# First u product of batch 2 split inside the last expert unit, tile 10 reordered, and the start of a fused attention and mixture-of-experts kernel rearranged

## The chip, the cores and the metric

The kernel runs on one core of one Trainium2 chip. The metric is the device time of one execution in microseconds (us). Engines are named as the profile names them: PE is TensorE, ACT is ScalarE, DVE is VectorE, POOL is GpSimd, SP the engine that issues most DMAs.

## What is computed

```python
xn = layernorm(x)                                  # x: 4 batches x 1024 tokens x 256
q, k, v = xn @ Wq.T + bq, xn @ Wk.T + bk, xn @ Wv.T + bv
qk = q @ k.T                                       # per batch, unscaled
theta = 0.5 + 0.2 * sigmoid(qk) + 0.15 * tanh(qk) + 0.1 * relu(qk)
s = (softmax(theta) @ v) @ Wo.T + bo
e = argmax(xn @ Wr + br)                           # one of 8 experts
y = gelu(xn @ W1[e] + b1[e]) @ W2[e] + b2[e]       # 256 -> 1024 -> 256
out = x + s * silu(y)
```

## The kernel before

**Work.** A tile is 128 tokens: 32 tiles, 8 to a batch. Large products are made of rounded parts, high and low: three matmuls (lines 899, 900, 901, in `product`) stand for one. `M` (from Wq and Wk) turns xn into u, and scores are u times xn; `G` (from Wv and Wo) turns xn into v. Every result of PE lands in one of eight banks of PSUM. ACT copies it out as the high part (`high_u`, `high_v`), DVE subtracts that to get the low part (`low_u`, `low_v`); only then may PE use it, or overwrite the bank.

**Stages.** (1) The start: DVE takes row statistics (`row_statistics`, `variances`, `scales`), three engines normalize tiles, PE turns them (`turn_0`), `first_u` makes u of batch 0, and the router's logits of batch 0 come from `route_0`. (2) Attention of batch 0, while the other batches are normalized on POOL, turned (`turn`) and routed. (3) Experts: the tokens, sorted by expert, pass in units of 256 rows. A unit that is at most half full takes another path: `half_rows`, `half_turned` and `half_out` on PE, `gelus_half` on ACT, `parts_half` on DVE. (4) Attention of batches 1 to 3, tiles 8 to 31, which begins inside the last units of the experts. In this execution the last unit (338 to 348.5 us) is a half one, and so is the only unit of expert 6 (304.4 to 313.9 us).

**A tile n of stage 4.** PE: `scores(n + 1)`; a wait for the low parts of tile n - 1's transposed weights (`pT_ready`); `transposes(n)`; a job; `weighted(n - 1)`, the product with v. ACT: six activations of tile n + 1 (`acts`), the transposed copy of tile n (`transposed_high`), two exponentials of tile n + 1 (`exps`), then the job's high part. DVE: `thetas(n + 1)`, `transposed_parts(n)`, the job's low part, and `finish(n - 1)`, which divides and frees the bank of `values`.

**Jobs.** `next_job(n)` gives for tile n a piece of the next batch's u (four) or v (four). All jobs of batches 2 and 3 use bank 7, so each waits until the piece before has both parts (`u_ready`). The first, for tile 9, is not run by the loop on PE but in the last expert unit, ahead of `half_turned`. Its parts, though, are made by the loop's turn of tile 9, behind `exps(10)` on ACT and `transposed_parts(9)` on DVE. The next job, of tile 10, waits for them.

**Order.** Every engine's program is written out by hand and runs in order; semaphores hold an instruction until its inputs are there, and all that stands behind it on that engine waits too. In the experts' stage each engine branches on the number of units, which it reads at run time.

Of the kernel before, what the change touches and what calls it, by code (L numbers as in the profile page):

```python
# [17 lines left out]
def block_attention_moe(nc, x, Wq, bq, Wk, bk, Wv, bv, Wo, bo, Wr, br, W1, b1, W2, b2, out):  # L18
# [34 lines left out]
    with ExitStack() as ctx:  # L53
# [496 lines left out]
        def _(act):  # L550
# [111 lines left out]
            act.wait_ge(scales_ready, 1)  # L662
            normalize(range(2))
            for m in range(DC):
# [130 lines left out]
            def units_of(e, u0, full, u1):  # L795
# [4 lines left out]
                with act.If(u0 < full):  # L800
                    gelus(u0, par)
                    row_high(u0 + 1)
                    high_w1(w1_landed, other, raw[0], slice(0, 1))
                with act.If(full < u0 + 1):
                    gelus_half(u0, par, beside=lambda: high_w1(w1_landed, other, raw[0], slice(0, 1)))
                    row_high(u0 + 1)
# [58 lines left out]
            with act.If(last_u < u7 + 2):  # L865
                tile_8()
            nc.scalar.activation(warm[:, 3:4], zeros[:, 0:1], ACT.Gelu)
            with act.If(last_u < full_7):
                gelus(last_u, 1)
            with act.If(full_7 < last_u + 1):  # L870
                gelus_half(last_u, 1)

# [7 lines left out]
            for n in range(TPB + 1, NT):  # L880
                if n + 1 < NT:
                    acts(n + 1, 0)
                    acts(n + 1, 1, beside=(lambda: transposed_high_0(NT - 2)) if n == NT - 2 else None)
                    transposed_high(n)
                    exps(n + 1)
                    job = next_job(n)
                    if job:
                        (high_u if job[0] == "u" else high_v)(*job[1:])
                    if n in ROWS_AT:
                        high_xT(3, [ROWS_AT.index(n)])  # L890
                else:
                    transposed_high(n)

        @block.tensor
        def _(pe):
# [225 lines left out]
            for m in range(DC):  # L1121
                for ec in range(DC):
                    last = mm(ps[:, 7, m * D:(m + 1) * D], wv_raw[:, ec, m * P:(m + 1) * P], woT[:, ec, :],
                              start=ec == 0, stop=ec == DC - 1)
                    if m == DC - 1 and ec == DC - 1:
                        last.then_inc(G_done, 1)
                    route_0(4 + 2 * m + ec)
            for ec in range(DC):
# [207 lines left out]
            for n in range(TPB + 1, NT - 1):  # L1336
# [3 lines left out]
                if n == TPB + 1:  # L1340
                    wait_apart(pe, y_biased, end_of[E - 1])
                    weighted(n - 1)
                    transposes(n)
                else:
                    pe.wait_ge(pT_ready, n * 2)
# [13 lines left out]
        def _(dve):  # L1359
# [137 lines left out]
            dve.wait_ge(scales_ready, 1)  # L1497
            normalize(range(2, 3))
            dve.wait_ge(x0_in[1], 16)
            statistics = row_statistics(range(4, TPB))  # L1500
            dve.wait_ge(biasT_done, 1)
            v.tensor_copy(bias_cols[:, :], ps[:, 6, BIAS_COL:BIAS_COL + 3 * DC]).then_inc(bias_kept, 1)
            step(statistics)
            variances(4, TPB)
# [57 lines left out]
            def take_turned(i):  # L1562
# [6 lines left out]

            thetas(0, [0])  # L1570
            dve.wait_ge(x_in[2], 16)
            row_statistics(range(2 * TPB, 2 * TPB + 2))
            dve.wait_ge(G_high, 1)
            v.tensor_tensor(G_lo[:, :, :], pair_of(ps[:, 7, :]), G_hi[:, :, :].bitcast(F32), ALU.subtract
# [11 lines left out]
                                   ).then_inc(const_kept, 1)  # L1586
            row_statistics(range(2 * TPB + 2, 3 * TPB))
            dve.wait_ge(x_in[1], 16)
# [165 lines left out]
            def first_unit_of(u, full, e, par):  # L1754

                other = 1 - par
                with dve.If(u < full):
                    hidden_parts(u)
                    row_low(u + 1)
                    low_w1(e, other, 0)  # L1760
                with dve.If(full < u + 1):
                    parts_half(u, beside=lambda: low_w1(e, other, 0))
                    row_low(u + 1)
# [80 lines left out]
            def job(n):  # L1844

                if next_job(n):
                    kind, b, q = next_job(n)
                    (low_u if kind == "u" else low_v)(b, q)
                if n in ROWS_AT:
                    low_xT(3, [ROWS_AT.index(n)])  # L1850

            thetas(TPB + 1)
            biased(last_u, 1)
# [68 lines left out]
```

## Time and profile before

| | us |
|---|---|
| median of 3 runs | 527.67 |
| lowest and highest | 527.51, 527.84 |
| the profiled execution | 527.64 |
| its span, first to last instruction | 525.6 |

| engine | busy us | share of the span |
|---|---|---|
| PE, matmuls | 515.6 | 98% |
| PE, weight loads | 484.3 | 92% |
| DVE | 402.6 | 77% |
| ACT | 344.6 | 66% |
| POOL | 195.8 | 37% |

A busy share is an average over all stages. Matmuls overlap, so a row's length is not its cost: a 128x512 matmul is shown with 0.39 us, but the next one starts 0.23 us later. Costs on PE are taken from start to start. PE's granted clock is 1.00 of full speed in every stretch used here.

### The profile page before, as it was taken

The page shows a single profiled execution, that of the slowest core. Times are in us where ns is not written, and L with a number is a line of the kernel's source. Part 1 is how long each engine was busy: PE and PEld are TensorE (multiplying, and loading weights), DVE is VectorE, ACT ScalarE, POOL GpSimd, SP SyncE. Part 2 cuts the span into 40 slices and gives each one's busy share as a digit, 9 for nine tenths or more (in the row PEclk, how much of TensorE's full clock was granted, in tenths as well). Part 3 has the DMA queues.
Part 4 walks back from the last instruction along what each step waited for, and adds up shares of the span by engine and source line. Part 5 has one row for each costly group of instructions (what it writes and reads, how often), then busy time and mean ns, then how long its engine had stood idle before and what let it go on. Part 6 is the DMA issues. An engine that isn't in the chain of part 4 may idle for free.

```text
span 525.6 us, 10829 instructions
## 1 busy us (share of the span) xinstructions
PE 515.6 (98%) x3773; PEld 484.3 (92%) x3773; DVE 402.6 (77%) x811; ACT 344.6 (66%) x633; POOL 195.8 (37%) x227
## 2 busy tenths in 40 slices
PE   7999999999999999999999989999999999999997
PEld 6899998899989999899999979998999989999997
DVE  5898689946578855598555688768999998867887
ACT  4789778437356733466343575899787786777884
POOL 3218419913112222222112222005676785342441
PEclk9999999999999999999999999999999999999999
DMA  8964720031635711247311421005233232211221
GB/s 266 344 225 176 285 81 1 2 120 32 230 123 151 255 55 41 61 133 237 112 40 40 136 70 42 21 22 190 62 99 113 71 114 87 62 44 49 60 71 51
DMA packets 40754, 57.49 MB, mean 109 GB/s; under 512 B 3654, under 2 KB 35788, under 8 KB 40156
## 3 DMA queue, kind: packets, MB, share of 16 engines
q1 hardware_dynamic: 35452, 46.02, 26.5%
q0 software_dynamic: 3488, 9.47, 6.4%
q10 hardware_dynamic: 1760, 1.32, 0.8%
q8 instruction: 28, 0.46, 0.4%
q14 instruction: 26, 0.21, 0.1%
HBM read 41.07 MB, written 17.56 MB: 112 GB/s over the span
## 4 chain that ended last, share of the span: by engine, by line
PE 86%; ACT 6%; DVE 5%; issue 1%; POOL 1%; DMA 1%; ACTq 0%; DVEq 0%
PE ps L899 26%; PE ps L901 25%; PE ps L900 25%; PE ps L1014 5%; DVE stats L1375 2%; PE ps L1193 1%; PE ps L1080 1%; ACT hid L763 1%; POOL xn_all L464 1%; DMA xn_all<-in_L_attn_x_dram 1%; PE ps L1070 1%; ACT relu_s L628 1%; ACT tanh_s L625 1%; ACT theta L624 1%; PE ps L1045 1%
## 5 line engine op out<-in xcount | busy, mean ns | idle before, releaser
L899 PE MATMUL ps<-v_hi,pT_hi 128*128 128x258 f32 x256 | 74.9, 293 | 0.2
L747 ACT ACTIVATE hid<-ps,b_now 128x256 f32<-128x256 f32 x128 | 53.7, 472 | 29.7 <-PE ps L901 28.8
L900 PE MATMUL ps<-v_lo,pT_hi 128*128 128x258 f32 x256 | 72.5, 283 | 0.0
L901 PE MATMUL ps<-v_hi,pT_lo 128*128 128x258 f32 x256 | 72.3, 282 | 0.0
L1430 DVE SCALAR_TENSOR_TENSOR theta<-tanh_s,theta 128x512 f32<-128x512 f32 x64 | 47.3, 739 | 23.5 <-ACT tanh_s L625 22.9
L899 PE MATMUL ps<-w_hi_even,hidT_h 128*128 128x256 f32 x200 | 58.5, 293 | 1.6 <-DVE hidT_l L1727 1.1
L636 ACT ACTIVATE theta<-theta,neg_max 128x512 f32<-128x512 f32 x64 | 43.0, 720 | 24.9 <-DVE neg_max L1436 24.6
L519 POOL COPY unit_token<-sorted_token 128x2 int32 x19 | 4.5, 238 | 142.9 <-PE ps L1193 142.9
L901 PE MATMUL ps<-w_hi_even,hidT_l 128*128 128x256 f32 x200 | 56.6, 283 | 0.0
L900 PE MATMUL ps<-w_lo_even,hidT_h 128*128 128x256 f32 x200 | 56.6, 283 | 0.0
L778 ACT ACTIVATE g_sb<-y_sb 128x512 f32<-128x512 f32 x20 | 12.6, 631 | 65.8 <-DVE y_sb L1742 65.8
L624 ACT ACTIVATE theta<-ps,c_half 128x512 f32<-128x512 f32 x64 | 44.3, 692 | 17.4 <-PE ps L901 17.3
L510 POOL DMA_INDIRECT row<-xn_rows,unit_token x38 | 44.1, 1161 | 20.7 <-POOL unit_token L519 14.9
L899 PE MATMUL ps<-xnT_hi,u_hi 128*128 128x512 f32 x128 | 51.7, 404 | 0.0
L526 POOL DMA_INDIRECT g_tile<-sorted_g,slot_g x32 | 37.5, 1171 | 38.0 <-DMA sorted_g<-g_sb 32.7
L901 PE MATMUL ps<-xnT_hi,u_lo 128*128 128x512 f32 x128 | 50.4, 394 | 0.0
L900 PE MATMUL ps<-xnT_lo,u_hi 128*128 128x512 f32 x128 | 50.0, 391 | 0.0
L899 PEld LDWEIGHTS ps<-v_hi,pT_hi 128*128 128x128 f32 x256 | 48.4, 189 | 1.7 <-issue 1.2
L901 PE MATMUL ps<-rowT_h,w_lo_even 128*128 128x256 f32 x176 | 49.8, 283 | 0.0
L899 PE MATMUL ps<-rowT_h,w_hi_even 128*128 128x256 f32 x176 | 49.8, 283 | 0.0
L900 PE MATMUL ps<-rowT_l,w_hi_even 128*128 128x256 f32 x176 | 49.8, 283 | 0.0
L900 PEld LDWEIGHTS ps<-v_lo,pT_hi 128*128 128x128 f32 x256 | 48.6, 190 | 0.3
(258 smaller groups left out, 1641.5 us busy)
## 6 DMA issues: line engine op xcount, KB each, us to landing
w_raw_odd<-in_L_ffn_W_dram SPq DMA_DIRECT2D x10, 1024.0 KB
w_raw_even<-in_L_ffn_W_dram SPq DMA_DIRECT2D x6, 1024.0 KB
sorted_g<-g_sb SPq DMA_DIRECT2D x20, 256.0 KB, 2.2
xn_rows<-xn_all SPq DMA_DIRECT2D x4, 1024.0 KB, 6.2
x_tile<-in_L_attn_x_dram SPq DMA_DIRECT2D x32, 128.0 KB, 2.2
out_dram<-g_tile SPq DMA_DIRECT2D x32, 128.0 KB, 1.7
xn_all<-in_L_attn_x_dram SPq DMA_DIRECT2D x3, 1024.0 KB, 12.4
kept_xT<-passing_xT SPq DMA_DIRECT2D x2, 1024.0 KB, 4.0
```

Source lines behind the costliest of these rows:

```text
L510: pool.indirect_dma_start(row[:, a, :], None, xn_rows, bass.IndirectOffsetOnAxis(ap=tokens[:, a:a + 1], axis=0)).then_inc(row_in, 16)
L526: pool.indirect_dma_start(g_tile[:, p % RING, :], None, sorted_g, bass.IndirectOffsetOnAxis(ap=slot_g[:, n:n + 1], axis=0)).then_inc(g_in[ ...
L624: nc.scalar.activation(theta[:, j % 2, cols], bank, ACT.Tanh, bias=c_half[:, n:n + 1], scale=0.5)
L636: nc.scalar.activation(part, part, ACT.Exp, bias=neg_max[:, j % 2, 1:2], scale=-1.0, accum_out=exp_sums[:, h:h + 1] if n == NT - 1 else No ...
L747: last = nc.scalar.activation(hid[:, j % 2, c * UNIT:(c + 1) * UNIT], ps[:, HID_BANK + j, c * UNIT:(c + 1) * UNIT], ACT.Gelu, bias=b1_now[ ...
L778: nc.scalar.activation(g_sb[:, :, :], y_sb[:, :, :], ACT.Tanh, scale=0.5).then_inc(y_tanh, 1)
L899: mm(dst, a_hi, b_hi, start=first, stop=False)
L900: mm(dst, a_hi, b_lo, start=False, stop=False)
L901: return mm(dst, a_lo, b_hi, start=False, stop=last)
L1014: last = nc.tensor.transpose(pT_bank(n, h)[:, i * P:(i + 1) * P], theta[:, n % 2, h * HALF + i * P:h * HALF + (i + 1) * P], ident[:, :])
L1375: last = v.bn_stats(stats[:, i, :], xn_all[:, i, :])
L1430: v.scalar_tensor_tensor(part, tanh_s[:, cols], KT, part, ALU.mult, ALU.add).then_inc(mixed, 1)
```

## The change

Six edits, no arithmetic among them.

1. The parts of job 9 (u of batch 2, piece 0): ACT's `high_u` goes into the last unit, in a half one between the copy of `hid` and the GELUs; DVE's `low_u` goes behind the last unit's parts, ahead of `thetas(9)`.
2. PE at tile 10: the job now stands ahead of the wait and of the transposes.
3. ACT and DVE at each expert's first unit: the second `If` becomes an `Else`.
4. The first rows: ACT normalizes tile 0 alone, DVE tiles 1 and 2 (it was 0 and 1, and 2). DVE's statistics of tiles 4 to 7 come behind the copy of the bias columns.
5. PE: the logits of tiles 4 to 7 come in one group behind all four products of `G`, whose semaphore is raised at the end of these.
6. DVE: statistics of two tiles of batch 2 move ahead of `thetas(0, [0])`, so that two fewer remain for later.

```diff
@@ ACT
-            normalize(range(2))
+            normalize(range(1))
...
-                with act.If(full < u0 + 1):
+                with act.Else():
                     gelus_half(u0, par, beside=lambda: high_w1(w1_landed, other, raw[0], slice(0, 1)))
...
+            def first_job():
+                high_u(*next_job(TPB + 1)[1:])
             with act.If(last_u < full_7):
                 gelus(last_u, 1)
+                first_job()
             with act.If(full_7 < last_u + 1):
-                gelus_half(last_u, 1)
+                gelus_half(last_u, 1, beside=first_job)
...
-                    if job:
+                    if job and n > TPB + 1:
@@ PE
-                    if m == DC - 1 and ec == DC - 1:
-                        last.then_inc(G_done, 1)
-                    route_0(4 + 2 * m + ec)
+            last.then_inc(G_done, 1)
+            for t in range(4, TPB):
+                route_0(t)
...
+                elif n == TPB + 2:
+                    job(n)
+                    pe.wait_ge(pT_ready, n * 2)
+                    transposes(n)
+                    weighted(n - 1)
@@ DVE
-            normalize(range(2, 3))
-            dve.wait_ge(x0_in[1], 16)
-            statistics = row_statistics(range(4, TPB))
+            normalize(range(1, 3))
             dve.wait_ge(biasT_done, 1)
             v.tensor_copy(bias_cols[:, :], ps[:, 6, BIAS_COL:BIAS_COL + 3 * DC]).then_inc(bias_kept, 1)
-            step(statistics)
+            dve.wait_ge(x0_in[1], 16)
+            step(row_statistics(range(4, TPB)))
...
-            thetas(0, [0])
             dve.wait_ge(x_in[2], 16)
             row_statistics(range(2 * TPB, 2 * TPB + 2))
+            thetas(0, [0])
+            row_statistics(range(2 * TPB + 2, 2 * TPB + 4))
...
-                with dve.If(full < u + 1):
+                with dve.Else():
...
-                if next_job(n):
+                if next_job(n) and n > TPB + 1:
...
+            low_u(*next_job(TPB + 1)[1:])
             thetas(TPB + 1)
```

What this does to the engines' programs at three places:

PE at tile 10, before. The rows are the end of `scores(11)`, the transposes (`ident,theta`), the job (`M_hi`, `M_lo`) and the first of `weighted(9)`.

```order
L901 MATMUL ps<-xnT_hi,u_lo 128x512
L1014 MATMUL ps<-ident,theta 128x128 x8
L899 MATMUL ps<-xnT_hi,M_hi 128x512
L900 MATMUL ps<-xnT_lo,M_hi 128x512
L901 MATMUL ps<-xnT_hi,M_lo 128x512
...
L899 MATMUL ps<-v_hi,pT_hi 128x258
```

The same place after:

```order
L905 MATMUL ps<-xnT_hi,u_lo 128x512
L903 MATMUL ps<-xnT_hi,M_hi 128x512
L904 MATMUL ps<-xnT_lo,M_hi 128x512
L905 MATMUL ps<-xnT_hi,M_lo 128x512
...
L1014 MATMUL ps<-ident,theta 128x128 x8
L903 MATMUL ps<-v_hi,pT_hi 128x258
```

The job's six matmuls moved ahead of the eight transposes.

ACT in the last unit and at tile 10, before: the half unit's copy, GELUs and parts; left out are tile 9's and tile 10's activations; then the exponentials of tile 10 and the high part of u.

```order
L757 ACTIVATE hid<-ps 128x512
L761 REGISTER_ALU
L763 ACTIVATE hid<-ps,b_now 128x128 x4
...
L636 ACTIVATE theta<-theta,neg_max 128x512 x2
L585 ACTIVATE u_hi<-ps,r_col 128x512
L624 ACTIVATE theta<-ps,c_half 128x512
```

The same places after:

```order
L757 ACTIVATE hid<-ps 128x512
L585 ACTIVATE u_hi<-ps,r_col 128x512
L761 REGISTER_ALU
L763 ACTIVATE hid<-ps,b_now 128x128 x4
...
L636 ACTIVATE theta<-theta,neg_max 128x512 x2
L624 ACTIVATE theta<-ps,c_half 128x512
```

`u_hi` moved from behind tile 10's exponentials to behind the half unit's copy.

DVE at the start, before: normalizing the first rows, the statistics of tiles 4 to 7, the copy of the bias columns, the variances.

```order
L1390 SCALAR_TENSOR_TENSOR shift<-mean_var,rstd 128x4
L1484 TENSOR_SCALAR xn_all<-xn_all,rstd,shift 128x256
L1375 BN_STATS stats<-xn_all 128x6 x4
L1502 COPY bias_cols<-ps 128x6
L1382 BN_AGGR mean_var<-stats 128x2 x4
```

After:

```order
L1399 SCALAR_TENSOR_TENSOR shift<-mean_var,rstd 128x4
L1493 TENSOR_SCALAR xn_all<-xn_all,rstd,shift 128x256 x2
L1509 COPY bias_cols<-ps 128x6
L1384 BN_STATS stats<-xn_all 128x6 x4
L1391 BN_AGGR mean_var<-stats 128x2 x4
```

One more tile is normalized here, and the four statistics moved behind the copy, which waits for a transpose of PE.

## Rows read from the trace of the kernel before

**Rows 1.** The page, busy time: us, share of the span, instructions.

```profile
PE 515.6 (98%) x3773; PEld 484.3 (92%) x3773; DVE 402.6 (77%) x811; ACT 344.6 (66%) x633; POOL 195.8 (37%) x227
```

**Rows 2.** Timeline of PE at tile 10: start, us, engine, line, instruction, idle before.

```profile
358.43 0.39 PE L901 MATMUL ps<-xnT_hi,u_lo 128*128 128x512 f32 x1
359.11 1.09 PE L1014 MATMUL ps<-ident,theta 128*128 128x128 f32 x8 [0.29 <-DVE pT_lo L1451]
360.63 0.50 PE L899 MATMUL ps<-xnT_hi,M_hi 128*128 128x512 f32 x1 [0.43 <-DVE u_lo L1410]
...
362.13 0.28 PE L899 MATMUL ps<-v_hi,pT_hi 128*128 128x258 f32 x1
```

**Rows 3.** Timelines of PE, ACT and DVE in the last unit, ACT at tile 10.

```profile
341.71 0.39 PE L901 MATMUL ps<-xnT_hi,M_lo 128*128 128x512 f32 x1
...
341.32 0.58 ACT L757 ACTIVATE hid<-ps 128x512 f32<-128x512 f32 x1
342.65 0.63 ACT L763 ACTIVATE hid<-ps,b_now 128x128 f32<-128x128 f32 x2 [0.75 <-PE ps L1248]
...
359.13 0.67 ACT L585 ACTIVATE u_hi<-ps,r_col 128x512 fp32r<-128x512 f32 x1
...
346.86 0.69 DVE L1430 SCALAR_TENSOR_TENSOR theta<-tanh_s,theta 128x512 f32<-128x512 f32 x1 [0.70 <-ACT tanh_s L625]
```

**Rows 4.** Timelines of DVE, POOL and PE around tile 11.

```profile
362.80 0.85 DVE L1430 SCALAR_TENSOR_TENSOR theta<-tanh_s,theta 128x512 f32<-128x512 f32 x1 [0.29 <-ACT tanh_s L625]
363.68 1.12 DVE L1436 CUSTOM_DVE_ANT_0 theta<-theta,relu_s,neg_max 128x512 f32<-128x512 f32 x1
...
365.44 1.29 DVE L1451 TENSOR_TENSOR pT_lo<-ps,pT_hi 128x512 fp32r<-128x512 f32 x2
366.79 0.75 DVE L1410 SCALAR_TENSOR_TENSOR u_lo<-ps,r_col,u_hi 128x512 fp32r<-128x512 f32 x1
...
362.03 1.07 POOL L543 TENSOR_TENSOR g_tile<-half_s,g_tile 128x256 f32<-128x256 f32 x1 [0.85 <-DMA g_tile<-sorted_g,slot_g]
363.18 1.07 POOL L546 TENSOR_TENSOR g_tile<-g_tile,x_tile 128x256 f32<-128x256 f32 x1
...
367.76 1.03 PE L1014 MATMUL ps<-ident,theta 128*128 128x128 f32 x8
368.55 0.48 PE L899 MATMUL ps<-xnT_hi,M_hi 128*128 128x512 f32 x1
```

**Rows 5.** Chain of waits at expert 6's half unit, then PE's timeline there.

```profile
306.93 0.04 ACTq L804
...
306.99 0.04 ACTq L804
...
310.52 0.38 PE L899 MATMUL ps<-w_hi_even,hidT_h 128*128 128x256 f32 x1 [1.10 <-DVE hidT_l L1727]
```

**Rows 6.** Timelines of DVE, POOL, PE and ACT at the start.

```profile
8.03 0.41 DVE L1484 TENSOR_SCALAR xn_all<-xn_all,rstd,shift 128x256 f32<-128x256 f32 x1
8.36 1.40 DVE L1375 BATCH_NORM_STATS2 stats<-xn_all 128x6 f32<-128x256 f32 x4
9.68 0.14 DVE L1502 COPY bias_cols<-ps 128x6 f32<-128x6 f32 x1
...
8.60 0.22 PE L915 MATMUL ps<-ident,bias_rows 6*128 6x6 f32 x1
9.18 1.09 PE L926 MATMUL ps<-ident,xn_all 128*128 128x128 f32 x8 [0.35 <-ACT xn_all L568]
...
10.92 1.17 PE L947 MATMUL ps<-xnT_hi,M_hi 128*128 128x512 f32 x4
...
10.52 0.58 ACT L657 ACTIVATE xnT_hi<-ps 128x512 fp32r<-128x512 f32 x1
```

**Rows 7.** Timelines of ACT and PE where batch 2 is first turned.

```profile
37.69 0.20 ACT L564 ACTIVATE std<-std 128x16 f32<-128x16 f32 x1
...
43.79 0.44 PE L1070 MATMUL ps<-ident,xn_all 128*128 128x128 f32 x2 [0.23 <-POOL xn_all L464]
```

More of the change, by code:

```diff
@@ L1586, in _ @@
                                    ).then_inc(const_kept, 1)
-            row_statistics(range(2 * TPB + 2, 3 * TPB))
+            row_statistics(range(2 * TPB + 4, 3 * TPB))
             dve.wait_ge(x_in[1], 16)
```

## The prediction

> **What bounds the kernel now.** I read the page first: PE is busy for 98% of the span [rows 1], so an edit gains only where PE stands still, or where it lets PE start sooner. Then the timelines of PE, from start to start, for the steps that are longer than their kind; then, at each of these, the timelines of the engines that release it, and the chain of waits.
>
> Five places matter. At tile 10 PE begins the last score matmul at 358.43 and the transposes at 359.11, where 0.23 us is the usual step; it waited for the low parts of tile 9. The transposes are followed by the job's first matmul at 360.63, which waited for `u_lo` [rows 2]. At expert 6's half unit PE resumes at 310.52 after over 1 us, at the end of a chain that passes through ACT's sequencer, branches among it [rows 5]. At the start PE waits 0.35 us until 9.18 for ACT's second normalized tile [rows 6]. At 43.79 it waits for POOL's rows of batch 2 [rows 7]. Between these PE runs from one matmul into the next.
>
> **Edits 1 and 2, the job of tile 10.** PE is free at 358.43 + 0.23 = 358.66. The parts of job 9 are then long made, and the job goes at once: 6 x 0.23 = 1.38, to 360.04. Its place also covers the wait for tile 9's low parts, which ended before 359.11 [rows 2]. Eight transposes take 368.55 - 367.76 = 0.79 [rows 4], to 360.83, and the first value matmul behind them costs some 0.08 more than one behind a job. Against 362.13 [rows 2] that is 362.13 - 360.91 = **1.22 us gained there**.
>
> What pays for it: in the last unit ACT copies `hid` at 341.32 for 0.58, then idles 0.75 until 342.65. Job 9's last matmul starts at 341.71 and ends at 342.10; a high part that starts then, and holds ACT for 0.57, ends at 342.71, so the GELUs start 0.06 later, not 0.57 [rows 3]. On DVE the low part (0.75, rows 4) meets 0.70 of idle ahead of `theta` at 346.86 [rows 3]: 0.05 more. Without these gaps the price would be 0.57 and 0.75 on a chain of ACT and DVE that has no other gap up to 359. ACT is later by 0.06 until tile 10's exponentials, and from 359.13 on, where `u_hi` stood, earlier by 0.57 - 0.06 = 0.51.
>
> What is late next is tile 11. PE now comes 1.22 sooner, ACT only 0.51. PE's transposes of tile 11 were at 367.76, now due at 366.54; the low parts that they need were ready at 365.44 + 1.29 = 366.73, and `u_lo` of the job behind them at 366.79 + 0.75 = 367.54, against a PE due at 367.33 [rows 4]. If DVE also came 0.51 sooner both would just fit, by 0.3. But DVE's second theta step, at 362.80, comes to 362.29, inside POOL's product of 362.03 to 363.10. Rows show what happens then: the reduction that begins at 363.68, inside POOL's sum of 363.18 to 364.25, takes 1.12 and ends 0.55 after the sum does [rows 4]. So the step would end at 363.10 + 0.55 = 363.65, the reduction start at 363.68 as before and end as before, and DVE would have gained nothing. PE then stands until 366.73 plus some 0.06: 0.25 given back, and `u_lo` at 367.54 to 367.60 costs nothing more. The bounds of the gain are 1.22 (nothing given back) and 0.95. I take 1.0, nearer to the overlap that the rows show. At tile 12 and behind, each turn of the loop gives PE more work than ACT and DVE, which catch up, so nothing more is lost.
>
> The Trainium skill, page "SBUF — State Buffer", section "SBUF: two separate sides", says that a DVE operation with two SBUF inputs and a GpSimd operation lock the shared ports for their whole length, the later one blocked fully. Worked out strictly, an operation of 0.69 would end 0.69 behind POOL's, not 0.55; by it tile 11 would give back about 0.4 and the sum below would be 0.15 less of a gain. No row here ends so late, and the rows' 0.55 decide.
>
> **Edit 3, `Else`.** At expert 6's half unit ACT's two sequencer rows of line 804, at 306.93 and 306.99, stand ahead of the copy that PE waits for [rows 5]. From the first of them to what follows the second is 0.13. They go, and ACT's copy, its split of the weights, DVE's split behind that and PE's restart at 310.52 all come **0.13 sooner**. DVE loses a like pair. In the other experts the first unit is full and PE waits for neither engine: zero there. Bounds: 0 to 0.16. The Trainium skill, page "Advanced Engine Details and Errata", section "Control Flow Timing", puts a compare-and-branch at about 108 ns; by it the term would be 0.11.
>
> **Edit 4, the first rows.** Sharing otherwise frees PE about 0.3 sooner than 9.18: ACT's one tile ends by about 8.6, DVE's two at 8.03 + 0.33 + 0.41 = 8.77. But DVE's statistics of tiles 4 to 7 began at 8.36; now they stand behind another tile and the bias copy, which needs PE's small transpose of 8.60 to 8.82 [rows 6]. The copy goes at about 8.87, the statistics at 8.98: **0.62 later**. Behind them, in order, are the variances, ACT's square root of group 1, and behind that on ACT the second `xnT_hi`, at 10.52 [rows 6], so at 11.14, ending at 11.72. PE's third matmul of `first_u` needs it. That one is the third of four from 10.92 to 11.92, at about 11.46; PE would be there at 11.15, and waits to 11.77. **PE is 0.3 late instead of 0.3 early**; bounds, the two signs. Statistics of the first group are not touched, and those of batch 3 wait for PE's turned rows anyway, so ACT and DVE follow PE, 0.3 late.
>
> **Edits 5 and 6.** Grouping changes no number of matmuls. The copy of `G` on ACT stands behind tile 0's activations, so the earlier semaphore buys nothing: 0, bounds -0.2 to 0.1. Two statistics less (2 x 0.33, rows 6) stand ahead of group 3, but its square root at 37.69 is ACT's, behind a table load, and follows ACT's own lateness [rows 7]. DVE's reciprocal can follow it more closely than before: 0.1. POOL's rows, and PE's 43.79, are then late by 0.3 - 0.1 = 0.2 and not 0.3, since PE waited there [rows 7]. **Start: 0.2 lost**; bounds, 0.4 lost to 0.3 gained.
>
> **Sum.** -1.0 - 0.13 + 0.2 = -0.93. Against the profiled execution: 527.64, span 525.6, would be 526.7, span 524.7. That execution is 0.03 below the median, so 527.67 - 0.93 = **526.7**. The end of the kernel is PE's, behind which only the last tile's gating stands, and comes sooner by the same.
>
> **Rivals.** (a) *The start gains.* PE starts 0.3 sooner and the statistics are in time, by an earlier copy or a third matmul that can wait. For: nothing waits on DVE there now. Against: ACT is in order, and the square root stands ahead of the second `xnT_hi`. It gives -1.0 - 0.13 - 0.3: 526.2, and with nothing given back at tile 11, 526.0. 0.17. (b) *Tile 11 takes the stall over.* DVE waits for the whole of POOL's operation and then needs its own 0.69, where the rows show 0.55, or POOL's operations fall so that they hold DVE twice more, 2 x 0.4 as in the row of 1.12 against 0.69: 526.9 to 527.3. For: three of DVE's operations near POOL's are long. Against: half of the overlap is there before too. 0.18. (c) *It doesn't do what it says*: the high part in the last unit finds no gap, PE's `scores` or `half_out` waits for the GELUs, and tile 10 gains only what the unit loses; with the start, 527.6 to 527.9. Against: the 0.75 gap is there. 0.09. (d) *Slower: the statistics fall far behind.* Each us that they start after 8.66 is a us of PE, since in the order of ACT and DVE all first rows hang on them. At a start of about 10.1 the gain elsewhere, 1.1, is spent; at 11.2, 528.8. For: they now hang on three small loads of biases. Against: PE itself took the bias rows at 8.60 in the trace. 0.06. The forecast has 0.50.
>
> **The numbers.** About 0.2%, 1.06 us, is what a measurement of this kernel can tell from no change. Faster needs less than 526.61, slower more than 528.73. The forecast's own spread, 526.4 to 527.0, lies to over a third below that bound (0.19), (a) wholly (0.17), (b) hardly (0.02): faster 0.38. Slower is (d) with some of (c): 0.06. Same 0.56. The range that leaves out 0.2, most of (c) and (d) and the low end of (a), is 526.0 to 527.4.
>
> **What would show it.** In the profile after: `M_hi` matmuls ahead of tile 10's transposes with no idle; `u_hi` within 342.1 to 342.8, and the GELUs not over 0.1 later; at tile 11 a PE wait of 0.1 to 0.4 for `pT_lo`; PE's restart in expert 6's half unit 0.13 sooner against its first hidden matmul; the statistics starting at about 9.0 and a new gap in PE near 11.2 to 11.8; the POOL wait near 43.8 shrunk, not gone. I am wrong if PE shows no gap at 11.2 (rival a), if tile 11 waits over 0.5 (b), or if the last unit is longer by over 0.3 (c).

## The result, and the profile after

The changed kernel takes 526.98 us in the median of 20 runs (525.96 to 527.91), the kernel before 527.66 us in 20 runs beside it (527.27 to 528.47): a ratio of 0.9986, 95% interval 0.9979 to 0.9992, 0.7 us less. A second comparison, further down, gave 526.76 against 527.57, 0.9986 again (0.9977 to 0.9995). The forecast was 526.7, from 526.0 to 527.4.

The profiled execution of the changed kernel took 527.91 us, well above that median, with a span of 526.1; that of before has 525.6. So its trace has to be read place by place, not by its end. The page's busy row, beside [rows 1]:

```profile
PE 516.8 (98%) x3773; PEld 485.0 (92%) x3773; DVE 403.7 (77%) x812; ACT 344.6 (66%) x632; POOL 194.8 (37%) x227
```

**The start.** Timelines of PE, DVE and ACT of the changed kernel, to be held against [rows 6] (columns as there):

```profile
6.50 2.99 PE L914 MATMUL ps<-wk_raw,wq_raw 128*128 128x256 f32 x8
9.42 0.22 PE L919 MATMUL ps<-ident,bias_rows 6*128 6x6 f32 x1
9.57 1.09 PE L930 MATMUL ps<-ident,xn_all 128*128 128x128 f32 x8
...
12.55 0.73 PE L951 MATMUL ps<-xnT_hi,M_hi 128*128 128x512 f32 x2 [0.53 <-ACT xnT_hi L657]
...
14.87 1.05 PE L930 MATMUL ps<-ident,xn_all 128*128 128x128 f32 x8
...
9.68 0.17 DVE L1509 COPY bias_cols<-ps 128x6 f32<-128x6 f32 x1 [0.88 <-PE ps L919]
9.76 1.40 DVE L1384 BATCH_NORM_STATS2 stats<-xn_all 128x6 f32<-128x256 f32 x4
...
11.81 0.20 ACT L564 ACTIVATE std<-std 128x4 f32<-128x4 f32 x1 [0.95 <-DVE std L1393]
11.92 0.58 ACT L657 ACTIVATE xnT_hi<-ps 128x512 fp32r<-128x512 f32 x1
```

The new gap in `first_u` is there, at the matmul and behind the copy that the prediction named. It is 0.70 beyond the usual step, not 0.3, because everything hangs on the bias transpose, and that goes at 9.42, not at 8.60. The eight weight products ahead of it take 2.92 us here and 2.10 in before: here five of the steps between them are 427 ns and a sixth 260, in before one is 427 and a second 286; the others are about 216. This is PE's clock, of which more in the last section.

**Expert 6's half unit**, timeline of PE, beside [rows 5]:

```profile
311.39 0.38 PE L903 MATMUL ps<-w_hi_even,hidT_h 128*128 128x256 f32 x1 [1.13 <-DVE hidT_l L1736]
```

From the unit's first row product (305.50, before 304.44) to this restart it is 5.89 us, before 6.08: 0.19 gained.

**The last unit**, timelines of ACT and DVE, beside [rows 3]; PE is 1.145 later here than before:

```profile
342.47 0.58 ACT L757 ACTIVATE hid<-ps 128x512 f32<-128x512 f32 x1
343.28 0.69 ACT L585 ACTIVATE u_hi<-ps,r_col 128x512 fp32r<-128x512 f32 x1 [0.23 <-PE ps L905]
343.87 2.17 ACT L763 ACTIVATE hid<-ps,b_now 128x128 f32<-128x128 f32 x8
...
347.28 0.74 DVE L1419 SCALAR_TENSOR_TENSOR u_lo<-ps,r_col,u_hi 128x512 fp32r<-128x512 f32 x1
348.07 0.69 DVE L1439 SCALAR_TENSOR_TENSOR theta<-tanh_s,theta 128x512 f32<-128x512 f32 x1
```

The GELUs are 343.87 - 342.65 - 1.145 = 0.07 later than in before, `theta` 348.07 - 346.86 - 1.145 = 0.06; the rest of both parts lies in gaps.

**Tile 10**, timeline of PE, beside [rows 2]:

```profile
359.60 0.40 PE L905 MATMUL ps<-xnT_hi,u_lo 128*128 128x512 f32 x1
359.83 0.39 PE L903 MATMUL ps<-xnT_hi,M_hi 128*128 128x512 f32 x1
...
361.20 1.03 PE L1018 MATMUL ps<-ident,theta 128*128 128x128 f32 x8
361.99 0.37 PE L903 MATMUL ps<-v_hi,pT_hi 128*128 128x258 f32 x1
```

Job, transposes and values follow one another without idle. PE was 1.145 late and is now 0.14 early: 1.28 gained at the first value matmul. The value stretch behind it gives back 0.115, most of it at its first step, which is 0.20 behind transposes and 0.12 behind a job.

The table holds marks of PE from the timelines of all traces, in us. Start: the second turn of first rows (`turn_0(2)`). t43: where batch 2 is first turned [rows 7]. Half unit: from its first row product to the restart. Expert 7: the 48 products of its first unit with `hidT`, the turned hidden values, as one stretch. Tiles 10, 11: from the end of that stretch to the transposes of tile 11.

| kernel | bias transpose | start | t43 | half unit | expert 7 | tiles 10, 11 | span |
|---|---|---|---|---|---|---|---|
| before | 8.60 | 13.68 | 43.79 | 6.08 | 5.83 | 41.88 | 525.6 |
| after | 9.42 | 14.87 | 44.84 | 5.89 | 6.11 | 40.72 | 526.1 |
| after, again | 8.12 | 14.05 | 43.98 | 5.89 | 6.09 | 40.67 | 524.7 |
| edits 1, 2 | 8.06 | 13.61 | 43.72 | 6.07 | 5.83 | 40.69 | 524.3 |
| edit 1 | 8.59 | 13.91 | 43.98 | 6.09 | 5.83 | 41.24 | 525.2 |
| edit 2 | 8.15 | 13.68 | 43.76 | 6.09 | 5.82 | 44.33 | 528.2 |
| edit 3 | 8.20 | 13.61 | 43.70 | 5.89 | 6.07 | 41.88 | 525.6 |
| edit 4 | 8.19 | 13.95 | 44.01 | 6.08 | 6.04 | 41.84 | 526.1 |
| all but edit 4 | 8.13 | 13.65 | 43.62 | 5.89 | 6.10 | 40.72 | 524.4 |
| same, 1 more | 9.36 | 14.02 | 43.94 | 5.90 | 5.82 | 40.69 | 523.9 |
| after, exchanged | 8.13 | 13.65 | 43.61 | 5.89 | 6.09 | 40.74 | 524.3 |
| same, 2 more | 8.68 | 13.60 | 43.53 | 5.90 | 5.85 | 40.69 | 524.1 |
| before, late | 9.36 | 14.01 | 44.09 | 6.08 | 5.82 | 41.85 | 525.8 |
| after, late | 10.52 | 15.97 | 45.90 | 5.89 | 6.10 | 40.72 | 526.6 |

### The profile page after: what moved, and what is told of

Same layout as the page of the kernel before. It is cut to its first block, busy times and chain, and to the rows that moved or that the text cites. A ratio compares the mean times of both kernels' runs of the same rounds, so it can differ in the third digit from the quotient of the medians.

```text
span 526.1 us, 10821 instructions
## 1 busy us (share of the span) xinstructions
PE 516.8 (98%) x3773; PEld 485.0 (92%) x3773; DVE 403.7 (77%) x812; ACT 344.6 (66%) x632; POOL 194.8 (37%) x227
## 4 chain that ended last, share of the span: by engine, by line
PE 86%; DVE 5%; ACT 5%; issue 2%; POOL 1%; ACTq 0%; POOLq 0%; DVEq 0%
PE ps L903 26%; PE ps L905 25%; PE ps L904 25%; PE ps L1018 5%; PE ps L1197 1%; PE ps L1084 1%; POOL xn_all L464 1%; DVE theta L1439 1%; DVE stats L1384 1%; ACT hid L763 1%; PE ps L910 1%; PE ps L1074 1%; DVE theta L1445 1%; ACT theta L624 1%; PE ps L1049 1%
## 5 line engine op out<-in xcount | busy, mean ns | idle before, releaser
L1439 DVE SCALAR_TENSOR_TENSOR theta<-tanh_s,theta 128x512 f32<-128x512 f32 x64 | 49.1, 767 | 22.5 <-ACT tanh_s L625 21.7
```

The costliest lines, as they stand in the source:

```text
L1439: v.scalar_tensor_tensor(part, tanh_s[:, cols], KT, part, ALU.mult, ALU.add).then_inc(mixed, 1)
```

## The experiments: the parts of the change alone

Each kernel was timed in five rounds beside the kernel before, whose median was 527.56 to 527.60 in all three comparisons.

**Edits 1 and 2 alone**, on the kernel before:

```diff
+            def first_job():
+                high_u(*next_job(TPB + 1)[1:])
...
-                gelus_half(last_u, 1)
+                gelus_half(last_u, 1, beside=first_job)
...
+                elif n == TPB + 2:
+                    job(n)
+                    pe.wait_ge(pT_ready, n * 2)
+                    transposes(n)
+                    weighted(n - 1)
```

> Edits 1 and 2 alone: job 9's parts in the last unit, tile 10's job ahead of its transposes; everything else as before. The theory of the prediction: 1.22 us gained at tile 10 (the pair of traces showed about 1.3), of which 0.25 is given back at tile 11 as a wait of PE for pT_lo (DVE inside POOL's operations): 1.0 us faster than before, bounds 0.95 to 1.3. If PE's stall at tile 11 takes more of it over, 0.3 to 0.7. If the last unit pays for it, 0. If the later gap that the trace of after shows at the first job of batch 3 (0.35 us) comes from these edits, the gain is about 0.7 and the same gap stands in this trace.

Measured: 526.57 against 527.56, ratio 0.9981 (0.9972 to 0.9990), 1.0 us faster. In the trace tiles 10 and 11 take 1.19 less, and the last unit costs PE nothing. So the gain of the change is here. By the medians the other four edits together lose 0.2 to 0.3 of it, which the intervals can't confirm.

**Edit 1 without edit 2**, the parts early, the job behind its transposes as before (the `elif` above left out):

> Edit 1 without edit 2: job 9's parts in the last unit, but tile 10's job behind its transposes as before. By the rows of before, PE still waits for the low parts until 359.11, but the job follows its transposes at 359.93 + 0.03 instead of 360.63: 0.67 gained at tile 10, of which tile 11 gives back little: 0.5 to 0.7 faster than before. If the job's place is worth nothing, 1.0 as with both edits; if the parts early are worth nothing, 0.

Measured: 526.93 against 527.57, 0.9988 (0.9979 to 0.9997), 0.6 us faster; by the table 0.64. PE's timeline at tile 10:

```profile
359.31 1.09 PE L1018 MATMUL ps<-ident,theta 128*128 128x128 f32 x8 [0.38 <-DVE pT_lo L1455]
360.16 0.48 PE L903 MATMUL ps<-xnT_hi,M_hi 128*128 128x512 f32 x1
```

The wait for `u_lo` of [rows 2] is gone, that for `pT_lo` stays. By the traces each of the two waits was worth about half, 0.64 and 0.55; the times alone (526.93 and 526.57, intervals that overlap) don't tell the two kernels apart.

**Edit 2 without edit 1**, the job ahead of the transposes, its parts late as before (the `elif` alone):

> Edit 2 without edit 1: tile 10's job ahead of its transposes, but job 9's parts still made behind tile 10's exponentials. By the rows of before the job's first matmul can't go until u_lo is ready, 360.63, and now the transposes, the low parts of tile 10 and the values stand behind it: PE waits once from 358.66 to 360.63, then job 1.37 and transposes 0.79 reach 362.79 where before had 362.13: 0.6 to 0.8 slower than before. If PE's bank or buffers let the job go earlier, faster.

Measured: 529.79 against 527.60, 1.0036 (1.0024 to 1.0048), 2.2 us slower, three times what was expected. PE's timeline, and a row of the windows view (stretch: us, busy us and count of PE, weight loads, DVE, ACT and POOL, granted clock, DMA share, GB/s):

```profile
360.56 0.50 PE L899 MATMUL ps<-xnT_hi,M_hi 128*128 128x512 f32 x1 [1.82 <-DVE u_lo L1415]
...
361.13 0.63 PE L901 MATMUL ps<-xnT_hi,M_lo 128*128 128x512 f32 x1
...
361.00:364.40 3.40, 3.40 (x14) 2.87 (x13) 3.04 (x6) 2.19 (x4) 2.05 (x4) 0.52 0.25 81
```

The restart is where it was expected, 360.56. But after 1.82 us of idle in one piece, and some 0.5 us behind the restart, the granted clock fell from 1.00 to the lower of PE's two levels (1.2 GHz; the view's stretch has a mean of 0.52), until about 364.5. Matmuls that step by 0.23 stepped by 0.43, and from the first of the eight transposes to the values it took 1.56 instead of 0.79. The places that in before idle for up to 1.10 [rows 5] show no such thing. Of the 2.45 us that the trace loses at tiles 10 and 11, then, some 0.7 is waiting and the rest the clock.

The clock did not fall in every execution. Of the six timed, four have a mean granted clock of 0.997 and took 529.65 to 530.17; two have 1.000 and took 528.55 and 528.85. All 25 executions of the kernel before have 0.999 or 1.000. So the median of 529.79 is that of executions with the fall; without it edit 2 alone costs 1.0 to 1.3 us, nearer to the 0.6 to 0.8 that were expected, and with it 2.1 to 2.6. Only one of the six has a trace, so that the other two had the same idle is not shown. By the traces edit 2 is worth 0.55 with edit 1 ahead of it.

**Edit 3 alone**, `Else` for the second `If`, on ACT and DVE:

```diff
-                with act.If(full < u0 + 1):
+                with act.Else():
...
-                with dve.If(full < u + 1):
+                with dve.Else():
```

> Edit 3 alone: Else in place of the second If, on ACT and DVE. Theory of the prediction: 0.13 us faster (0 to 0.16), PE's restart in expert 6's half unit 0.13 to 0.19 sooner against the first hidden matmul of the unit, and nothing anywhere else. Rival, from the trace of after: the other layout of ACT's instructions makes one gate read late, a new wait of PE for hidT_l near 323 in expert 7's first unit costs 0.28, and the edit by itself is 0.1 us slower. If the new wait is absent here, it came from elsewhere or by chance.

Measured: 527.76 against 527.56, 1.0004 (0.9995 to 1.0013): nothing that can be told. The trace shows both halves, +0.24 and -0.19. PE's timeline in the half unit, 0.19 shorter from its first row product:

```profile
304.31 0.40 PE L899 MATMUL ps<-w_hi_even,rowT_h 128*128 128x512 f32 x1
...
310.21 0.39 PE L899 MATMUL ps<-w_hi_even,hidT_h 128*128 128x256 f32 x1 [1.14 <-DVE hidT_l L1727]
```

And expert 7's first unit takes 6.07 instead of 5.83. Where that comes from stands below, in the section on ACT's sequencer.

**Edit 4 alone**, the first rows:

```diff
-            normalize(range(2))
+            normalize(range(1))
...
-            normalize(range(2, 3))
-            dve.wait_ge(x0_in[1], 16)
-            statistics = row_statistics(range(4, TPB))
+            normalize(range(1, 3))
             dve.wait_ge(biasT_done, 1)
             v.tensor_copy(bias_cols[:, :], ...)
-            step(statistics)
+            dve.wait_ge(x0_in[1], 16)
+            step(row_statistics(range(4, TPB)))
```

> Edit 4 alone: ACT normalizes tile 0 only, DVE tiles 1 and 2, then the bias copy, then the statistics of tiles 4 to 7. Theory of the prediction: 0.3 us slower, by a new stall of PE in the third matmul of first_u. The trace of after showed that stall (0.7 us) and, since PE's clock rose later there, turned tiles 0.4 later: if the statistics hang on PE's bias transpose, then in this trace the stall is 0.3 when the first eight weight products run mostly at 216 ns and the bias transpose goes at about 8.6, and 0.7 or more when it goes at 9.4; in the median 0.3 to 0.8 slower. Rival a: 0.3 faster, no stall.

Measured: 528.58 against 527.56, 1.0018 (1.0009 to 1.0027), 1.0 us slower. PE's timeline of the profiled execution, which took 527.79, less than the median:

```profile
8.19 0.22 PE L915 MATMUL ps<-ident,bias_rows 6*128 6x6 f32 x1
8.96 1.06 PE L926 MATMUL ps<-ident,xn_all 128*128 128x128 f32 x8 [0.56 <-DVE xn_all L1484]
...
11.63 0.73 PE L947 MATMUL ps<-xnT_hi,M_hi 128*128 128x512 f32 x2 [0.23 <-ACT xnT_hi L657]
```

With the transpose at 8.19 the step is 0.41 too long. The turned rows start at 8.96, where the traces without edit 4 and an early transpose have 9.10 to 9.18: the new share frees PE 0.1 to 0.2 sooner, not 0.3, since DVE's two tiles took 0.90. Net 0.27 to 0.34 late at `turn_0(2)`. This trace also has the longer stretch in expert 7 (6.04), and 0.2 at the first job of batch 3, of which more below. Its span is 0.5 over that of before; the other half of the 1.0 us was lost in executions that have no trace.

**All but edit 4**:

> All edits of the change but edit 4: the start is shared as before, the statistics stand ahead of the bias copy. If edit 4 costs 0.3 to 0.8, this kernel is faster than before by 1.1 to 1.3 us less what the later gaps at expert 7's first unit (0.28) and at the first job of batch 3 (0.35) take, and faster than after by what edit 4 costs. If edit 4 gains 0.3 it is slower than after by that.

Measured: 526.42 against 527.56, 0.9979 (0.9969 to 0.9989), 1.1 us faster than before. That is 0.3 to 0.6 faster than the whole change, too little beside the intervals to be told from it by time alone; its trace has no gap in `first_u`. The two measurements of edit 4, 1.0 alone and about 0.5 in company, overlap within their intervals.

## The experiments: what the start hangs on

**The changed kernel again**, unaltered:

> The changed kernel once more, unaltered, as the yardstick of this comparison and to see what of its first trace comes back. Expected: 0.5 to 0.9 us faster than before. The time at which PE's clock rises may differ; the stall of first_u is 0.4 where the bias transpose goes at about 8.2 and 0.7 where it goes at 9.4. The extra 0.3 us in ACT's sequencer near 316 should come back between the same two instructions of line 792 if it belongs to the program, and anywhere or nowhere if it is chance; with it the hidden products of expert 7's first unit take 6.1 instead of 5.83.

Measured: 526.76 against 527.57, 0.9986 (0.9977 to 0.9995), and a profiled span of 524.7. The transpose went at 8.12 and the step was 0.42 too long; the longer stretch in expert 7 was there again (6.09), between the same two instructions of ACT; the gap at 416 was not.

**ACT's pair exchanged**, on the changed kernel:

```diff
             high_xT_0(0)
-            square_root(1, slice(4, TPB))
             high_xT_0(1)
+            square_root(1, slice(4, TPB))
             act.wait_ge(scales_ready, 2)
```

> The changed kernel with one pair of ACT's instructions exchanged: the second xnT_hi ahead of the square root of group 1, so that PE's third matmul of first_u no longer hangs on the statistics. Theory (the new stall is this order of ACT): the stall goes whole (0.4 to 0.7), first_u runs through, the rows of group 1 are ready at about the time PE asks for them, and this kernel is 0.5 to 0.9 faster than after; start 0.2 to 0.3 earlier than before at turn_0(2). Rival: the rows of group 1, behind the late statistics, become the wait at turn_0(2), and only 0.1 to 0.3 is gained.

Measured: 526.36 against 527.57, 0.9978 (0.9968 to 0.9988), 0.4 faster than the changed kernel in the same comparison. PE's and ACT's timelines:

```profile
9.16 1.06 PE L930 MATMUL ps<-ident,xn_all 128*128 128x128 f32 x8 [0.81 <-DVE xn_all L1493]
...
10.87 1.19 PE L951 MATMUL ps<-xnT_hi,M_hi 128*128 128x512 f32 x4
...
9.82 1.08 ACT L657 ACTIVATE xnT_hi<-ps 128x512 fp32r<-128x512 f32 x2 [0.53 <-PE ps L930]
```

`first_u` runs through: the stall was this order of ACT, and group 1's rows are in time at `turn_0(2)`. That is 0.40 sooner than in the unaltered kernel by the traces, just under what the theory had, with no wait at `turn_0(2)` in its place (the times differ by as much, but their intervals overlap); and it is no sooner than before (13.65 against 13.68): the share of the first rows is worth nothing by itself, for PE now waits for DVE instead of ACT.

**The bias transpose later**, in the kernel before and in the changed one:

```diff
+            for _ in range(6):
+                mm(ps[:, 6, 0:P], ident[:, :], ident[:, :], start=True, stop=True)
             pe.wait_ge(small_in, 16 * 3)
```

> The kernel before with six small matmuls more (0.11 us each at PE's full clock, 0.21 at half) between PE's weight products and its bias transpose, so that the transpose is 0.64 later at full clock. Theory: in before nothing but the bias copy hangs on it and the statistics stand ahead of that copy, so PE's 0.8 us of idle ahead of turn_0(0) takes it: 0 to 0.1 slower. Rival: whatever delays PE here delays all, 0.6 slower.

> The changed kernel with the same six small matmuls. Theory: the statistics of tiles 4 to 7 hang on the bias copy, so they, the square root, the second xnT_hi and PE's third matmul of first_u come later by what the bias transpose ends after DVE's second normalized tile (the copy goes 0.6 later at most): the stall of first_u grows from 0.4 to about 0.9 and the kernel is 0.4 to 0.6 slower than after. Rival: no more than before loses by it.

Measured: before with them 528.51 against 527.60, 1.0016 (1.0007 to 1.0025), 0.9 slower; after with them 528.08 against 527.60, 1.0010 (1.0000 to 1.0019), about 1.2 slower than after without, which was timed in other comparisons. As times they don't part the two theories, because I had sized the delay wrongly: the six are twelve rows of the trace and take 1.43, not 0.64, which is more than the idle of before. PE's timelines, before late and then after late:

```profile
7.93 1.50 PE L914 MATMUL ps<-ident 128*128 128x128 f32 x12
9.36 0.22 PE L917 MATMUL ps<-ident,bias_rows 6*128 6x6 f32 x1
```

```profile
10.52 0.22 PE L921 MATMUL ps<-ident,bias_rows 6*128 6x6 f32 x1
...
12.41 0.72 PE L953 MATMUL ps<-xnT_hi,M_hi 128*128 128x512 f32 x2
```

The traces do part them, with the table. Without edit 4, `turn_0(2)` stands at 13.6 to 13.7 for transposes up to 8.6 (the trace of edit 1 alone, 13.91, is the one exception, with turned rows at 9.40; DVE's first normalized tile is at 8.26 in it, in before at 8.03), and 4.65 behind the transpose where that comes at 9.36, in two traces. With edit 4 as written it is 5.45 behind it, at 9.42 and at 10.52, and 14.0 where it goes at 8.1 to 8.2. So edit 4 costs 0.3 to 0.4 where the transpose is early and 5.45 - 4.65 = 0.80 where it is late. The theory that before loses nothing by a late transpose holds only up to about 9.0.

## The experiments: 0.3 us in ACT's sequencer

In before, ACT's gate of expert 7's first unit (`g_sb`, line 778) starts 1.41 behind the start of the small copy of line 787; in the changed kernel 1.76. The timelines of ACT, before and then after:

```profile
314.88 0.20 ACT L787 ACTIVATE b_now<-b_cols 128x8 f32<-128x8 f32 x1
316.29 0.63 ACT L778 ACTIVATE g_sb<-y_sb 128x512 f32<-128x512 f32 x1 [1.21 <-DVE y_sb L1742]
```

```profile
315.77 0.19 ACT L787 ACTIVATE b_now<-b_cols 128x8 f32<-128x8 f32 x1
317.53 0.63 ACT L778 ACTIVATE g_sb<-y_sb 128x512 f32<-128x512 f32 x1 [1.58 <-DVE y_sb L1751]
```

The releaser named had long been done: between the two stand only sequencer instructions, two register loads with the arithmetic behind them (lines 792 and 793 of the kernel before). One step between neighbours is 0.3 longer than its like. With edit 3 or edit 4 it is the step behind the first register load (0.60 against 0.31), with both it is one instruction further (0.48 against 0.18, in both traces of the changed kernel and at the same spot). Each of these edits takes an instruction out of ACT's stream ahead of it, so I put them back as tiny activations where ACT idles.

**Two tiny activations at ACT's start**, on the kernel with the exchanged pair:

```diff
             nc.scalar.activation(warm[:, 0:1], zeros[:, 0:1], ACT.Sqrt)
+            nc.scalar.activation(warm[:, 4:5], zeros[:, 0:1], ACT.Sqrt)
+            nc.scalar.activation(warm[:, 5:6], zeros[:, 0:1], ACT.Sqrt)
```

> As the run with the exchanged pair, and two tiny ACT activations more at the very start, where ACT idles. Theory: an extra 0.3 us of ACT's sequencer sits at a fixed count of instructions in its stream; edits 3 and 4 each take one instruction out ahead of expert 7, which moves it from a place where ACT waits anyway to one ahead of the gate. Two instructions more put it back: the extra time is gone from line 792, the hidden products of expert 7's first unit take 5.83 instead of 6.1, 0.2 to 0.3 faster than without the two. Rival: it depends on something else, 6.1 as before and the same time.

**One tiny activation** on the kernel without edit 4:

> All edits but edit 4 and one tiny ACT activation more at the very start (edit 3 alone takes one instruction out, so one puts the extra 0.3 us of ACT's sequencer back). Theory of the fixed count: the extra time is gone from line 792, the hidden products of expert 7's first unit take 5.83 and not 6.10, 0.2 to 0.3 faster than without it, 526.1 to 526.3. Against the kernel with the exchanged pair and two activations it tells what the new share of the first rows is worth once its stall is gone: by the traces 0 to 0.1.

Measured: 525.81 against 527.57, 0.9971 (0.9960 to 0.9983), and 526.18 against 527.60, 0.9974 (0.9964 to 0.9985). That is 0.55 and 0.24 below the same kernels without pads (526.36 and 526.42), within the intervals, so the traces have to decide. ACT's timelines at the gate, of the exchanged pair without pads, with two, and of all but edit 4 with one:

```profile
316.18 0.63 ACT L778 ACTIVATE g_sb<-y_sb 128x512 f32<-128x512 f32 x1 [1.56 <-DVE y_sb L1751]
```

```profile
315.88 0.63 ACT L780 ACTIVATE g_sb<-y_sb 128x512 f32<-128x512 f32 x1 [1.27 <-DVE y_sb L1753]
```

```profile
316.33 0.63 ACT L779 ACTIVATE g_sb<-y_sb 128x512 f32<-128x512 f32 x1 [1.27 <-DVE y_sb L1753]
```

The idle is 0.29 shorter, and PE's stretch is 5.85 and 5.82 again, where it was 6.09 and 6.10: an activation of 0.2 us added in an idle place at the start takes 0.25 us off a unit 310 us later. Seven traces lack the extra time and seven have it, and all fourteen fit one fixed place in ACT's program. It is not a fixed number of instructions that ran: ahead of the small copy 645 rows of ACT ran both with edit 4 alone, which shows the extra time, and in the two kernels with pads, which don't (before 646, edit 3 alone 644). So instructions that are jumped over must count too; that edit 3 is worth one place is inferred from where the long step lies.

Is it the fetch of instructions? No row of ACT says so, but the DMA view counts packets of instructions. Its row of queue 14 (packets, MB, share) for 315.5 to 317.5, in the kernel before and with edit 3 alone:

```profile
q14 instruction: 1, 0.01, 1.7%
```

```profile
q14 instruction: 2, 0.02, 2.5%
```

In each of the seven traces without the extra time one packet of this queue starts 2.4 to 2.7 us ahead of the small copy, and one 1.7 to 2.0 behind it. In each of the seven with it there is none ahead, and two come 1.5 to 2.1 behind it. So with the extra time a fetch of instructions has moved there too. It starts 0.6 us or more behind the end of the long step, so the step isn't a wait for that packet to land, and what ACT does in it is not shown. Nor does the view name the engine that a packet is for: that the moved one is ACT's, and that the long step belongs to it, is inferred from the split of the fourteen traces. The Trainium skill, page "Runtime: NRT & Kernel Launch", section "Instruction fetch mechanics", says that an engine's instructions are refilled in blocks of fixed size while it runs, and that the cost of crossing into the next block is mostly hidden; these traces fit the first, and here the cost is not hidden.

These two are the fastest kernels of the study, by point estimate 0.6 to 1.0 below the changed kernel's median in the same or a neighbouring comparison. Between them nothing can be told. In the trace of the one with a single activation the stretch from tile 11 to the end is 0.5 or more shorter than in every other, by 0 to some 0.07 a tile; I didn't find out why.

## The forecast, step by step

**The sum was right, and partly by luck.** In the trace of the changed kernel with an early transpose (after, again) PE is 0.37 late at the start, 0.15 late at the half unit, 0.04 early behind it, 0.22 late behind expert 7's first unit, 0.98 early at tile 11, and the span ends 0.9 sooner. The forecast was a span of 524.7, and that span is 524.7. But two terms were wrong and cancel: tiles 10 and 11 gave 1.21 instead of 1.0, and edit 3, forecast to gain 0.13, came with a loss of 0.07 (0.19 gained in expert 6, 0.26 lost in expert 7). The start's 0.15 by the half unit is the 0.2 of the forecast. The median came 0.3 above it, at 526.98. That fits a start that costs more in other executions, as in the first trace: the 20 times of the changed kernel spread over 1.95 us, those of before over 1.2. But only profiled executions have traces, so it is not shown.

**Tile 10: 1.22 forecast, 1.28 to 1.31 found at the first value matmul.** The forecast had taken off 0.08 for the values behind transposes, and that comes only behind this matmul, as 0.115; like for like, at the transposes of tile 11, it is 1.14 to 1.21. The last unit pays 0.07 on ACT and 0.06 on DVE, forecast 0.06 and 0.05. The two gaps of [rows 3] took the parts as reckoned, and rival (c) is out.

**Tile 11: 0.25 given back forecast, 0 to 0.05 found.** This is the step that failed. I let DVE's second theta step come sooner, as it did, but left POOL's product of [rows 4] where it was. Timelines of DVE, POOL and PE of the kernel without edit 4, which is 0.12 ahead of before up to there:

```profile
362.13 1.18 DVE L1439 SCALAR_TENSOR_TENSOR theta<-tanh_s,theta 128x512 f32<-128x512 f32 x1 [0.38 <-ACT tanh_s L625]
363.34 1.11 DVE L1445 CUSTOM_DVE_ANT_0 theta<-theta,relu_s,neg_max 128x512 f32<-128x512 f32 x1
...
365.09 1.29 DVE L1460 TENSOR_TENSOR pT_lo<-ps,pT_hi 128x512 fp32r<-128x512 f32 x2
...
362.02 0.74 POOL L543 TENSOR_TENSOR g_tile<-half_s,g_tile 128x256 f32<-128x256 f32 x1 [0.94 <-DMA g_tile<-sorted_g,slot_g]
...
366.44 1.08 PE L1018 MATMUL ps<-ident,theta 128*128 128x128 f32 x8
```

DVE's step starts at 362.13, inside POOL's product, and ends 0.55 behind it, just as the rows of before had it: 362.76 + 0.55 = 363.31. But the product is 0.74 long now and not 1.07, for in before it started beside a reduction of DVE's (361.81 to 362.50), so the reduction starts 0.22 sooner than I had it, and the low parts are ready at 366.38, as PE arrives. Of two engines that hold each other up, both move. Rival (b) is out. The rule of the Trainium skill that I weighed there (page "SBUF — State Buffer", section "SBUF: two separate sides": the later operation is fully blocked, so 0.69 behind POOL's end) isn't what this row shows either: 0.55 again.

**Edit 3: 0.13 forecast, 0.19 found at its place**, just over the bound of 0.16, and "zero there" for the other experts was wrong by 0.25: not by a wait or branch that `Else` changes there, but by where the instructions behind it lie in ACT's program. Both together come to nothing in the kernel's time.

**Edit 4: 0.3 late forecast, 0.3 to 0.4 found with an early transpose, 0.8 with a late one.** Mechanism, matmul and copy were right, and rival (a) is out. Mis-sized was what the statistics hang on: I took the bias transpose at 8.60 as given. In the twelve traces without added work it goes at 8.06 to 9.42, and and by the 5.45 of the table each 0.1 of it beyond about 8.6 is 0.1 of PE. That is rival (d) in small, with PE's clock at the start as its cause, not the loads. The 0.3 that the new share was to free was 0 to 0.2 (turned rows at 8.96 to 9.16 in the four traces with it and an early transpose, 9.10 to 9.18 without, the exception above left out), DVE's two tiles taking 0.90 where I had added up 0.74, and the exchanged pair shows that nothing of it reaches `turn_0(2)`.

**Edit 6: 0.1 absorbed forecast, 0.14 found.** From the start mark to t43 it is 30.06 to 30.11 in the seven traces without it and 29.92 to 29.97 in the seven with it. These seven have edit 5 as well, which was not tried apart, so the 0.14 is that of both.

**Not forecast: a gap at 416.** In the first trace of the changed kernel PE waited 0.35 at the first job of batch 3; timelines of DVE and PE:

```profile
415.19 1.23 DVE L1412 TENSOR_TENSOR xnT_lo<-own_xT,xnT_hi 128x1024 fp32r<-128x1024 f32 x1 [0.25 <-ACT xnT_hi L604]
...
416.47 0.51 PE L903 MATMUL ps<-xnT_hi,M_hi 128*128 128x512 f32 x1
```

The low rows end at 416.41, and the job goes behind them. DVE is 0.35 later than in before from 391 on, where a theta step of 0.87 became one of 1.22 beside one of POOL's operations; POOL's next ones, which follow DVE, are later too and meet it again at each tile, while PE notices nothing for 25 us. The trace of edit 4 alone has 0.2 there, the second trace of the same changed kernel none. So it isn't fixed by the program; that it goes by how the two engines happen to meet is my reading of these rows.

## What to carry to other kernels

Before a step is moved ahead of a wait, ask whether what it needs can be ready: by the traces the job's place was worth 0.55 us with its parts early, and with them late it cost 1.0 us or more, and over 2 where PE's clock fell as well. An instruction that waits for another engine should stand behind, not ahead of, work that others wait for; ACT's one exchanged pair took back what the changed statistics cost. Where DVE and POOL hold each other up, move both in the estimate, and where an engine runs close to its due time, look at more than one trace before reading a gap of 0.3 as the work of an edit.

## What the runs showed of the hardware

- **PE's clock at the start rises at another time in each execution.** PE works from 2.9 on in all fourteen traces. The first products of weights step by 427 ns or by 216, and the eight take from 1.8 to 2.9 us. A step of 427 is what the run of edit 2 shows at a granted 0.52. The windows view prints 1.00 there in either case, but only because no record of the clock covers the stretch: each trace's first record of the full clock starts at 5.80 to 8.72 us, where its steps halve (8.72 in the first trace of the changed kernel, 7.07 in before, 6.07 in the second of the changed kernel). The Trainium skill, page "TensorE: Matmul & The Clock Gate", section "Part 1: The HAM clock gate (the "warmup" mystery)", puts the spread of this change at half a microsecond to either side from run to run, and warns in the same section that the number of slow matmuls of one kernel varies; here the change lay between 5.8 and 8.7, nearly three microseconds apart.
- **An idle of 1.82 us inside the work was followed by the lower clock** (a mean of 0.52 over the next 3.4 us), in the one trace that has it; the mean clock says the same of four of that kernel's six executions and not of two. Idles of up to 1.14 in the fourteen traces were not.
- **About 0.3 us of ACT's sequencer at a fixed place in its program**, visible only where ACT is late: taking out one or two instructions ahead brought it into the open, one or two more activations at the start hid it.
- A two-input operation of DVE (the theta step) or its reduction that starts inside one of POOL's ends 0.55 behind it, in the rows shown.
